# An audio tower on one core: GpSimd takes over the slot columns of two batches and the weighing of exponentials, with a reordered tail

## What is computed

```python
h = batchnorm(conv3(sign(x), sign(kernel)))            # 748 tokens of 64 features
q, k, v = split(layernorm(h) @ Wqkv + bqkv)            # 8 heads
attn = softmax(q·k / 8, over the axis of queries)
h = h + (diag(attn) * v) @ W0 + b0                     # only the diagonal of attn is used
y = layernorm(h)
# fast feed-forward: a tree of depth 7; at each of 8 levels
#   score = y·w1[node] + b1[node];  node = 2*node + 1 + (score > 0)
#   out += gelu(|score|) * (y @ w2[node] + b2[node])
h = h + out
```

## Time and profile before

| | us |
|---|---|
| median of 3 runs | 474.37 (473.8 to 483.96) |
| the profiled execution | 474.62 |
| its span | 472.7 |
| busy: TensorE, VectorE, ScalarE, GpSimd | 352.7, 342.5, 324.0, 284.2 |
| mean granted TensorE clock | 0.911 |

### The profile page before, as it was taken

One profiled execution on the slowest core, in us unless ns is written; L12 is line 12 of the kernel. 1 busy time (PEld: TensorE's weight loads), 2 busy tenths in 40 slices (PEclk: granted clock), 3 DMA queues, 4 the chain that ended last, 5 costly groups with the idle time before them and its releaser, 6 DMA issues.

```text
span 472.7 us, 8346 instructions
## 1 busy us (share of the span) xinstructions
PE 352.7 (75%) x2606; PEld 248.5 (53%) x2606; DVE 342.5 (72%) x577; ACT 324.0 (69%) x832; POOL 284.2 (60%) x398
## 2 busy tenths in 40 slices
PE   1156896878789889777898769883512999999970
PEld 1144565655456555445664446552312777788860
DVE  0475969899788878998888998978530789955440
ACT  1363996788888998577898656758200799987760
POOL 4315748786867875584689662661552365666663
PEclk9996999989999999989999999995555999999995
DMA  4425243417998972131243130018915012120000
GB/s 95 128 62 136 53 113 81 101 39 172 178 187 160 151 182 47 53 97 29 71 113 97 38 82 1 3 42 116 118 31 139 23 36 56 33 54 6 12 15 5
DMA packets 58953, 37.27 MB, mean 79 GB/s; under 512 B 31661, under 2 KB 57607, under 8 KB 58906
## 3 DMA queue, kind: packets, MB, share of 16 engines
q1 hardware_dynamic: 54778, 33.81, 35.7%
q0 software_dynamic: 3328, 2.36, 2.0%
q10 hardware_dynamic: 800, 0.49, 0.5%
HBM read 11.42 MB, written 7.50 MB: 40 GB/s over the span
## 4 chain that ended last, share of the span: by engine, by line
DVE 33%; issue 17%; ACT 15%; PE 15%; POOL 12%; DMA 5%; SPq 1%; POOLq 0%; DVEq 0%; ACTq 0%
DVE nm L1392 14%; ACT Z L1192 10%; POOL out L726 8%; PE Z L923 6%; POOL pre L723 3%; DMA pre<-in_x 3%; DVE va L1421 2%; ACT q L1134 2%; DVE pre L1488 2%; ACT k L1134 1%; PE Z L843 1%; DMA pool_a<-pool_a 1%; DVE pre L1503 1%; DVE va L1437 1%; DVE pre L1665 1%
## 5 line engine op out<-in xcount | busy, mean ns | idle before, releaser
L1192 ACT ACTIVATE Z<-Z,nm 125x748 f32<-125x748 f32 x192 | 166.3, 872 | 61.5 <-DVE nm L1392 60.2
L1392 DVE TENSOR_REDUCE nm<-Z 125x1 f32<-125x748 f32 x192 | 175.4, 933 | 36.4 <-PE Z L923 30.0
L923 PE MATMUL Z<-pool_a 128*125 128x512 f16 (+1 forms) x768 | 162.0, 338 | 28.1 <-ACT Z L1192 23.4
L923 PEld LDWEIGHTS Z<-pool_a 128*125 128x125 f16 x768 | 87.7, 140 | 71.8 <-ACT Z L1192 46.0
L726 POOL DMA_INDIRECT out<-pre,va x44 | 44.7, 1017 | 35.1 <-POOL pre L723 35.1
L1665 DVE TENSOR_REDUCE pre<-va 128x64 f32<-128x512 f32 x44 | 45.7, 1039 | 5.8 <-ACT va L1275 2.4
L790 PE MATMUL Z<-xhT,wq 128*128 128x249 f16 (+1 forms) x192 | 32.9, 291 | 11.9 <-DVEq L1402 10.5
L1192 ACT ACTIVATION_READ_ACCUMULATOR Z<-Z,nm 125x1 f32 x192 | 41.2, 215 | 0.0
L652 POOL DMA_INDIRECT sorted_rows<-xrow,slot x24 | 30.4, 1266 | 15.3 <-DVE slot L1544 8.7
L620 POOL TENSOR_TENSOR va<-va 125x256 f32<-125x256 f32 (+2 forms) x54 | 29.6, 548 | 10.3 <-DVE va L1421 7.2
L596 POOL TENSOR_TENSOR pool_a<-q,pool_a 128x748 f16<-128x748 f32 x15 | 24.7, 1644 | 10.2 <-DVE pool_a L1349 9.1
(11 more groups left out here) (243 smaller groups left out, 667.1 us busy)
## 6 DMA issues: line engine op xcount, KB each, us to landing
pool_a<-pool_a SPq DMA_DIRECT2D x64, 187.0 KB, 3.3
pool_a<-pool_a SPq DMA_DIRECT2D x64, 93.5 KB, 2.2
sorted_rows<-zrow SPq DMA_DIRECT2D x1, 3640.0 KB, 23.8
va<-sorted_rows SPq DMA_DIRECT2D x12, 260.0 KB, 3.0
w<-in_L_ffn_w2s SPq DMA_DIRECT2D x1, 2048.0 KB, 16.5
pre<-in_x SPq DMA_DIRECT2D x4, 375.0 KB
pool_a<-in_L_ffn_w2s SPq DMA_DIRECT2D x1, 1024.0 KB
out<-pre,va POOLq DMA_INDIRECT x44, 2.2
```

Of the source, the lines that this page charges most:

```text
L923: last = mm(z[0:XP, c0:c1], kst[:, u % 3, a, hd, KST[t]:KST[t] + XP], qst[:, u % 3, hd, c0:c1], start=(a == 0), stop=(a == 1))
L1192: sc_.activation(z, z, ACT.Exp, bias=nm[0:XP, u % 4, i:i + 1], accum_out=sm[0:XP, u % 4, i:i + 1]).then_inc(s_exp, 1)
L1392: v.tensor_reduce(nm[0:XP, u % 4, i:i + 1], Z[n % 3][0:XP, 0:N], X, ALU.max, negate=True).then_inc(s_max, 1)
```

## The change

GpSimd gets four new functions. `weights(w)` does the product of `diag_weights` for w = 0 to 11, in unit w + 1 behind `qk_lo`; VectorE keeps the reciprocal, and `weigh_heads` and `exps` wait for the new semaphore. For batches 0 and 1 `leaf_terms`, `group_terms` and `slot_terms` do the work of `leaf_counts`, `rank_of_token` and most of `group_slots` and `slots`; VectorE keeps the scan and what reads PSUM (`group_columns`, `slot_columns`), and the fills "pf" and "sl" move from (1, 10) and (2, 9) to (2, 2) and (3, 2). The memset of w7 is cut in five, in units 5 to 9; `leaf_columns` moves from unit 4 to unit 10 and SyncE's load of the table's bias row from unit 7 to unit 13. The first two pairs of the last batch are weighed together (`two_pairs_out`, `weigh_two`, `add_two`). In the tail the last diagonal is written to Z[0] right behind the last scores, VectorE's work is put in another order, and `own_slots(3)` stands ahead of `low_columns`. In the expert stage GpSimd adds the residual of tile k + 1 before it issues the rows of tile k; for overflow tiles VectorE adds it.

```diff
@@ fills
-            if 1 <= u <= NU and i < 3:
+            if 1 <= u < NU and i < 3:
                 f.append(("d", u - 1, i))
             if u == NU - 2:
-                f += {4: [("yp", LASTB, 0)], 6: [("yp", LASTB, 1)], 8: [("yp", LASTB + 1, 0)],
-                      10: [("yp", LASTB + 1, 1)]}.get(i, [])
+                f += {7: [("yq", 0)], 9: [("yq", 1)], 11: [("yq", 2)]}.get(i, [])
             if 1 <= b < B - 1:
-                f += {(0, 8): [("A", b - 1, 0)], (0, 10): [("A", b - 1, 1)], (1, 10): [("pf", b - 1)],
-                      (2, 9): [("sl", b - 1)]}.get((ph, i), [])
+                f += {(0, 8): [("A", b - 1, 0)], (0, 10): [("A", b - 1, 1)], (2, 2): [("pf", b - 1)],
+                      (3, 2): [("sl", b - 1)]}.get((ph, i), [])
             if b == B - 1:
-                f += {(0, 0): [("A", b - 1, 1)], (0, 5): [("yp", NU - 1, 0)], (0, 6): [("yp", NU - 1, 1)],
-                      (0, 8): [("pf", b - 1)], (0, 10): [("sl", b - 1)], (1, 0): [("t", b, 0)], (1, 1): [("t", b, 1)],
-                      (1, 2): [("L", b, 0)], (1, 3): [("L", b, 1)], (1, 5): [("A", b, 0)], (1, 6): [("A", b, 1)],
+                f += {(0, 0): [("A", b - 1, 1)], (0, 1): [("yp", NU - 1, 0)], (0, 2): [("yp", NU - 1, 1)],
+                      (0, 8): [("pf", b - 1)], (1, 0): [("t", b, 0)], (1, 1): [("t", b, 1)], (1, 2): [("L", b, 0)],
+                      (1, 3): [("L", b, 1)], (1, 4): [("sl", b - 1)], (1, 5): [("A", b, 0)], (1, 6): [("A", b, 1)],
                       (2, 0): [("pf", b)], (2, 2): [("sl", b)]}.get((ph, i), [])
@@ GpSimd: new functions
+            def weights(w):
+                pool.wait_ge(s_rc, w + 1)
+                pool.wait_ge(s_ex, w + 1)
+                gp.tensor_tensor(at[0:XP, w % 8], at[0:XP, w % 8], sm[0:XP, w % 4], ALU.mult).then_inc(s_atp, 1)
+                pool.wait_ge(s_atp, w + 1)
+            def leaf_terms(b):
+                pool.wait_ge(s_rk, b + 1)
...
+                link(gp.tensor_tensor(col[:, c_new0], col[:, c_cnt], Ct[:, NIN - 1:NIN], ALU.add))
...
+                pool.sem_inc(s_dg, 1)
+                gp.tensor_tensor(Xt, Ct, mT, ALU.mult).then_inc(s_xt, 1)
+                pool.wait_ge(s_xt, b + 1)
...
+            def slot_terms(b):
...
+                pool.wait_ge(s_sc, b + 1)
+                for n in range(2):
+                    link(gp.tensor_tensor(e[:, :, n], z[:, :, 0], z[:, :, 2 + n], ALU.subtract))
+                    link(gp.tensor_scalar(e[:, :, n], e[:, :, n], 0.0, 1.0, ALU.is_ge, ALU.mult))
+                    link(gp.tensor_tensor(e[:, :, n], e[:, :, n], z[:, :, 4 + n], ALU.mult))
+                link(gp.tensor_tensor(slf[0:XP], z[:, :, 1], e[:, :, 0], ALU.add))
+                for n in range(1, 3):
+                    link(gp.tensor_tensor(slf[0:XP], slf[0:XP], e[:, :, n], ALU.add))
+                gp.tensor_copy(slot[0:XP, bt], slf[0:XP]).then_inc(s_slot, 1)
@@ GpSimd: the loop over u, behind qk_lo(u + AHEAD)
-                if u == 4:
+                if ZERO_AT <= u < ZERO_AT + ZPARTS:
+                    pool.wait_ge(s_prod, u + AHEAD + 1)
+                    leaf_zeros(u - ZERO_AT)
+                if u == ZERO_AT + ZPARTS:
                     leaf_columns()
+                if 1 <= u <= LASTB:
+                    weights(u - 1)
+                if 1 <= b < B - 1 and ph == 1:
+                    leaf_terms(b - 1)
+                if 1 <= b < B - 1 and ph == 2:
+                    group_terms(b - 1)
                 if 0 <= b < B - 1 and ph < 2:
                     for t in range(3 * ph, 3 * ph + 3):
                         add_heads(b, t)
-                if u == NU - 2:
-                    add_pair(LASTB)
                 if 0 <= b < B - 1 and ph == 2:
                     ln2_squares(b)
                 if b >= 1 and ph == 3 and b < B - 1:
+                    slot_terms(b - 1)
                     own_slots(b - 1)
-                if NU - 2 <= u < NU:
+                if u == NU - 2:
+                    add_two()
+                if u == NU - 1:
                     add_pair(u - 1)
@@ GpSimd: expert stage
-                pool.wait_ge(s_yo, k + 1)
+            def rows_out(k):
+                if k < ST_TILES:
+                    pool.wait_ge(s_yo, k + 1)
+                else:
+                    pool.wait_ge(s_yov, k - ST_TILES + 1)
...
+            residual(0)
             for k in range(ST_TILES):
+                if k + 1 < ST_TILES:
+                    residual(k + 1)
                 rows_out(k)
@@ VectorE
             def weigh_heads(b, t):
                 k = NT * b + t
-                dve.wait_ge(s_at, NPAIR * (b + 1))
+                dve.wait_ge(s_atp, NPAIR * (b + 1))
-                    if 1 <= u <= NU and i == (7 if u < NU else 5):
+                    if 1 <= u <= NU and i == (7 if u < NU else 1):
                         diag_weights(u - 1)
-                    if 1 <= b < B - 1 and (ph, i) == (1, 1):
-                        leaf_ranks(b - 1)
-                    if 1 <= b < B - 1 and (ph, i) == (1, 3):
-                        leaf_counts(b - 1)
-                    if 1 <= b < B - 1 and (ph, i) == (1, 5):
-                        rank_of_token(b - 1)
+                    if 1 <= b < B - 1:
+                        if (ph, i) == (1, 1):
+                            leaf_ranks(b - 1)
@@ VectorE: tail, step 8 of unit NU
                         last_heads(NU - 1)
                         ln2_sums(B - 1)
                         ln2_last()
+                        leaf_counts(B - 2)
+                        old_terms()
+                        ln2_last_x()
                         rank_of_token(B - 2)
-                    if u == NU and i == 9:
-                        ln2_last_x()
@@ VectorE: overflow tiles
                         weigh(k)
                         sum_levels(k)
+                        add_residual(k)
```

More of the change, by code:

```diff
@@ L51 @@
 BIG = 1 << 20
+ROUND = 1.5 * 2.0 ** 23
 LN_EPS, BN_EPS = 1e-5, 1e-3
@@ new lines, in group_terms @@
+            def group_terms(b):
+                pool.wait_ge(s_gc, b + 1)
+                link(gp.tensor_tensor(col[:, c_new], col[:, c_new], col[:, c_cap], ALU.subtract))
+                link(gp.tensor_tensor(leaf[:, 4:5], col[:, c_last], col[:, c_j32], ALU.subtract))
+                link(gp.tensor_tensor(leaf[:, 5:6], col[:, c_new], col[:, c_last], ALU.subtract))
+                if b:
+                    pool.wait_ge(*full(("sl", b - 1)))
+                link(gp.tensor_copy(leaf16[:, 0, :], leaf[:]))
+                gp.tensor_tensor(leaf16[:, 1, :], leaf[:], leaf16[:, 0, :], ALU.subtract).then_inc(s_vn, 1)
+                pool.wait_ge(s_vn, b + 1)
+                link(gp.tensor_scalar(col[:, c_up], col[:, c_dn], 0.0, 1.0, ALU.is_gt, ALU.mult))
+                link(gp.tensor_tensor(col[:, c_up], col[:, c_up], leaf[:, 5:6], ALU.mult))
+                link(gp.tensor_tensor(col[:, c_last], col[:, c_last], col[:, c_up], ALU.add))
@@ L857, in pair_out, with two_pairs_out @@
                     last = mm(zt, pick[:, g, 0:XP], cb[:, js], start=False, stop=True)
+                last.then_inc(s_full, 1)
+            def two_pairs_out(n):
+                z = take(("yq", n))
+                for t in range(2 * n, 2 * n + 2):
+                    r0, g = v_tile(B - 1, t)
+                    zt = z[0:XP, t % 2 * 2 * P:(t % 2 + 1) * 2 * P]
+                    for a in range(2):
+                        mm(zt, xhT[:, r0:r0 + XP], mw[:, a, g * H * D:g * H * D + 2 * P], start=(a == 0), stop=False)
+                    last = mm(zt, pick[:, g, 0:XP], cb[:, 0:2 * P], start=False, stop=True)
                 last.then_inc(s_full, 1)
@@ L934, in fill @@
                     heads_out(f[1], f[2])
+                elif kind == "yq":
+                    two_pairs_out(f[1])
                 elif kind == "yp":
@@ L984, in _ @@
                         scores(u, i)
+                    if (u, i) == (NU - 1, 2 * NT - 1):
+                        for n in range(3):
+                            diagonal(u, n)
                     for f in fills(u, i):
@@ L1069, in _ @@
             early = [load_leaves(k) for k in range(ST_TILES, ST_TILES + EARLY)]
+            pe.wait_ge(s_tab, 16 * 2)
+            pe.wait_ge(s_low, 16 * 2 * sum(2 ** (lvs[-1] - lv) for _, lvs in LOW for lv in lvs))
+            pe.wait_ge(s_wc, 2)
+            pe.wait_ge(s_zl, LOWZ + 1)
             xs_T(0)
@@ L1555, in take @@
                     weigh_heads(f[1], f[2])
+                elif kind == "yq":
+                    weigh_two(f[1])
                 elif kind == "yp":
```

162 lines of the change are left out of this document (121 added, 41 removed).

## The result

The changed kernel took 492.86 us (median of 4 runs, 490.64 to 496.04), the kernel before 475.46 beside it: ratio 1.035, 95% interval 1.029 to 1.042. It is slower by 17 us, where 477.5 was forecast and 485 was the upper end. The profiled execution took 494.71, its span 493.0. The busy times explain little of it: VectorE 327.7 us (342.5 before), GpSimd 297.1 (284.2), TensorE 363.8 (352.7). Most of the time is in waits and in TensorE's clock.

The account below looks back on a forecast made before the run. The prediction saw no single bounding engine: the chain is spread over all, with VectorE, ScalarE and TensorE in lockstep in the loop. Its terms summed to +2.9 on 474.6, giving 477.5 us, range 466 to 485.

Parts of the forecast that it names:

- Unit 1: Zeros memset cut in parts, so VectorE's long operation under it shortens: -2.2 us.
- collisions: Units 2 and 3: VectorE's weights product no longer collides with GpSimd's reads: -0.8 us for both.
- units 4 and 7: VectorE waits for GpSimd's weights in unit 4, +1.1 us, and for its LayerNorm 2 squares in unit 7, +1.3.
- rival (b): GpSimd's small dependent operations cost 0.45 us each instead of 0.275, giving 484.6 to 486 us; chance 0.12.
- Unit 8, +4.7: VectorE's weighing waits for GpSimd's weights, queued behind its product and a part of the zeros: +4.7 us.
- unit 12, +7.7: VectorE's weighing waits for GpSimd, late from slot terms, scatters and products: +7.7 us.
- Units 9 to 11, +1.8: Slot columns leaving VectorE relieve 5.5 us, but its wait for GpSimd's late squares in unit 11 makes it +1.8.
- Units 13 to 15, -4.8: VectorE's relief stays, up to 7.0 us, less TensorE's wait for ln2_x in unit 15: net -4.8, bounds -7.0 and 0.
- Tail, -1.9: Earlier scan of batch 2 and LayerNorm 2 ahead of slot work: 1.9 of 3.6 us reach the last scan.
- the end, -4.0: Expert stage: last output DMA starts at 461.75 instead of 465.79, soon after VectorE's last sum: -4.0 us.
- The term of 0.85 "to wake GpSimd": End of the expert stage: 0.85 us between VectorE's last residual and GpSimd's last DMA.
- The static tiles, 0: Expert stage, first 32 tiles: GpSimd's period falls from 2.13 to 1.65 us, which hardly matters for the end.

Follow-up runs that it names:

- experiments 4 and 5: Kernel before plus VectorE memsets: 16 in each of units 8, 10, 12, lumped 501.32 us, spread 494.55; or 2, 4, 8, 12 in units 6 to 12, 491.26.
- experiment 8: Changed kernel, weights back on VectorE, GpSimd's squares ahead of the group's terms, zeros and add_two moved: 478.03 us; further reorderings 467.5, 468.12 and 466.81.
- experiment 6: Kernel before with only the expert stage changed: 469.95 us; beside it, reruns of the changed kernel, 486.18, and of it with weights back on VectorE, 466.98.

## Why the forecast was wrong, step by step

In the profile the change cost 17.4 us more than the sum of the forecast. By the table that is 1.4 in unit 8, 4.6 in units 9 to 11, 2.3 in unit 12, 3.6 in units 13 to 15 and 5.4 in the static tiles; the rest cancels. The waits were foreseen. What failed is the step from a wait to its price, and the size of the relief in units 13 to 15. The share of the static tiles has no known cause.

- **Unit 1, collisions, units 4 and 7**: right within 0.2 us each. The price of GpSimd's small operations (0.19 and 0.08 of gap) held too, so rival (b), which wanted 0.45, did not happen.
- **Unit 8, +4.7, and unit 12, +7.7**: the waits were 4.61, as worked out, and 8.52, 0.8 more. Mis-sized was the step from a wait to its cost: the prediction took "a stall of VectorE there is paid whole" for the whole price, and it was paid with TensorE's clock on top, 1.4 us at once in each (experiments 4 and 5). Of the 14 us (17 in the profiled execution) that the weights alone cost, the same working gives 8.3.
- **Units 9 to 11, +1.8, measured +4.1 and +6.4**: the forecast had 5.5 of relief and then 7.3 paid at unit 11. The relief was 4.3 (1.9 where the half clock behind unit 8 lasted into unit 9), the payment 8.4: the wait for the squares of 5.6, as the start of GpSimd's work said, and 2.7 behind it at clock 0.50, which stood in no term. A second consumer was missed as well: TensorE's slot fill at step 2 reads GpSimd's group terms. In after it waits 2.34 us beside the longer wait and costs nothing; it became the bound as soon as the squares went first (3.35 us, experiment 8).
- **Units 13 to 15, -4.8, measured -1.2 and +0.6**: by step 6 of unit 14 the relief had come (-4.3 and -4.2). What failed is the step at unit 15: "TensorE's transposes wait for ln2_x" was named and its bound of 0 given, but the sum took only 2.2 of the possible 7.0 off for it. The wait is there in after (2.41 us, TensorE's L980 at 325.81), and 3.1 and 4.8 us went back.
- **Tail, -1.9 (-2.5 and -2.7) and the end, -4.0 (-4.1)**: right within 0.8. GpSimd's period in the static tiles is 1.52 us in the median (1.65 was said), with a gap of 0.17 instead of 0.79; the end:

```profile
484.05 1.01 DVE L1832 TENSOR_REDUCE pre<-va 128x64 f32<-128x512 f32 x1
485.09 0.23 DVE L1838 TENSOR_TENSOR pre<-pre,va 128x64 f32<-128x64 f32 x1
486.11 0.97 POOL L818 DMA_INDIRECT out<-pre,va  x1 [2.61 <-DVE pre L1838]
```

  against the last two rows, the DMA now starts 1.05 us behind the sum's end instead of 5.15. The term of 0.85 "to wake GpSimd", for which no row was given, measured 0.79 (486.11 - 485.09 - 0.23).
- **The static tiles, 0, measured +5.4 in the first profile**: hold-ups that are not in the sum and of unknown cause; without them the same kernel took 486.2, still 8.7 over the forecast and beyond its range.
- **The rule on the shared port** (the Trainium skill, Perfetto Trace Analysis, "Optimizing Scalar/DVE Operations"): the forecast's 0.8 stayed, but new collisions came beside it, such as VectorE's product of unit 13 (L1528 in after), 1.48 us beside GpSimd's subtraction where its like takes 0.17. The trace agrees, with small sums.
- The rival on the other side (b) had the right sign and a wrong mechanism. That a wait lowers the clock was no rival at all, though the clock row of before, nearly all 9s in the loop, showed what there was to lose. Its price for the dearer case, 0.45 us, was called "still below a 125x64 addition with its gap (0.47)"; in before such an addition takes 0.32 us and the next one starts 0.40 behind it. The sum for unit 12 has a slip of 0.1 us: 263.3 - 253.69 is 9.6.

## What to carry to other kernels

In a loop that three engines run in lockstep, a wait can cost its length and the clock: waits and stalls of 0.7 to 2.1 us cost about their length here, those of 3.0 us and more 1.4 us or more beyond it. So ask what TensorE does meanwhile, and what its next steps take at half clock. When work moves to an engine with a serial queue, write down for every result who reads it and when, and where in the queue it stands: here products of 0.2 us cost 19 us behind the wrong neighbour and about 2 ahead of it. A stall that is removed uncovers the next consumer of the same queue, so follow it to the end of the kernel before taking the gain.

## What the runs showed of the hardware beyond what was expected

Of the doses, those of 0.66 and 1.45 us left the granted clock at 1.00, those of 3.01 and 4.58 took it to 0.50; behind the wait of unit 8 in after it stayed there for 15 us, and in the same kernel's other profile it was back at 1.00 within 10. Eight stalls of 0.66 us spread over a unit lowered it as well. It also fell where no stall came before: to 0.62 in units 10 and 11 of the unchanged loop of experiment 6, and to 0.56 between two doses. Why there is open. ScalarE can stand for 1.2 to 3.75 us with its input ready, released by something the profile calls "remote"; it was seen only in kernels with the new expert stage, on four of six occasions, and no run here tells its cause.
